# ScalarE's order in the slots that hold a z step: decays, then every z, then back

## The chip, the core and the metric

The kernel runs on one core of a Trainium2 chip. The metric is the device time of one execution in microseconds (us). Five engines work side by side, each through its own list of instructions in order: TensorE (PE, matrix products), VectorE (DVE), ScalarE (ACT), GpSimd (POOL) and SyncE (SP), whose list here is the issue of the DMA transfers. They meet only at semaphores: an instruction that waits holds back everything behind it on its engine.

## The reference, cut to what matters

The input is 64 series of 750 numbers. Each is cut into 10 patches of 128 (hop 64), so there are 640 tokens. All of this is computed, in this order:

```
h  = patches @ W.T + b
hn = rmsnorm(layernorm(h))
z, x, B, C, dt = split(hn @ in_proj.T)
dt = softplus(dt @ dt_proj.T + bias);  dA = exp(dt * A);  dBx = dt * x * B
state = dA * state + dBx               # along the 10 tokens of a series, 16 states per channel
y  = (sum over states of C * state) + D_skip * x
y  = y * silu(z);  m = res + y @ out_proj.T
h  = h + m + (silu(gate) * up) @ down  # on rmsnorm(m)
h  = h + second MLP on layernorm(h)
```

## The kernel before, in words

The tokens are cut into two chunks of 290 (chunk 0) and 350 (chunk 1); channels lie on the 128 partitions in 8 tiles. Everything is fp32. The recurrence is cut into 64 units: units 0 to 31 are chunk 0, units 32 to 63 chunk 1; four units make one tile of channels, and a unit holds four states. Units are the slots of the program: `schedule()` puts other steps beside each unit, and each engine walks the slots on its own.

What one unit costs each engine:

- ScalarE computes four decays `exp(dt*A)` (`decay`, L551) into the four PSUM buffers `da`. The buffers form a ring: decays 0 and 1 of a unit may be written once VectorE has finished the first product (L792) of the unit before, decays 2 and 3 once it has finished the second.
- GpSimd multiplies `dtx` and `bb` (L453) into `hs`; VectorE scans (L781) twice, multiplies by `cb` (L792), scans twice, multiplies. For chunk 0 TensorE then sums the states with an identity matrix (L1000, `state_sum`); for chunk 1 GpSimd adds them.
- After four units VectorE's `gate_y` (L807 and L813 in chunk 0, L810 and L813 in chunk 1) multiplies y by z. It waits for the state sum and for z.

Beside the units of chunk 0 run the projections of its own tiles and then those of chunk 1; beside the units of chunk 1 runs the first half of the work behind the recurrence for chunk 0 (output projection, two MLPs). Products go to a ring of three work banks of PSUM, later four: a product can start once the bank three products back has been read. ScalarE does the steps `dtp` (softplus), `xs`, `in_c` and `in_z` one slot late (`late(slots, 1)`). `in_z` is `silu`, from another table set than `exp`; `preload_act_table_set` loads a set (L528), and where a function of another set follows without one, a load appears at that function's own line (L551, L668).

ScalarE's loop over the slots (around L720) does, for each unit: decays 2 and 3 of this unit, the steps in `first`, decays 0 and 1 of the next unit, the steps in `second`, and a reload of the exp/log set if silu's is in. Where the slot holds `dtp`, `xs` or `in_c`, these are split between the two lists. Where it holds none, `second` is cut in half. That rule meets slots with z alone (4, 8, 12, 24, 28, 32: three z in the first, two in the others) and slots with z beside steps of another kind (37: `rms2` of chunk 0, `ysum` and the z of tile 6; 50: `ln2_mean`, on which ScalarE does nothing, and the z of tile 7). TensorE does slot 37's `rms2` product first in its slot, then that z's product, and then the first MLP; VectorE does `rms2`'s scaling (L864) between its scans.

SyncE issues the loads of `bb` and `cb` two and three units ahead, each when its buffer is free; those of the streamed weights `wraw` begin in slot 30 of its list.

Of the kernel before, what the change touches and what calls it, by code (L numbers as in the profile page):

```python
# [147 lines left out]
def late(slots, lag, kinds=LATE):  # L148
    def lag_of(i, s):
        if i == 1:  # L150
            return min(lag, 2)
        return lag if s[0] in kinds and slots[i][0] is not None and not (s in SEAM and lag == 1) else 0
    return [(unit, [s for j in range(max(0, i - lag), i + 1) for s in slots[j][1] if lag_of(j, s) == i - j])
            for i, (unit, _) in enumerate(slots)]
# [30 lines left out]
def build(nc, patches, tok_w, small, w_in, w_dt, w_stream, out):  # L185
    slots = schedule()
    uses = work_bank_uses()

    readers = [s for _, steps in slots for s in steps if s[0] in ("out", "gu", "down")]
    load_of = {s: i for i, s in enumerate(readers)}  # L190
    split_loads = [i for i, s in enumerate(readers) if s[0] != "out" and s[1] == NCH - 1]
# [4 lines left out]
    with ExitStack() as ctx:  # L196
# [137 lines left out]
        def splits_at(s):  # L334
            if s == ("out", NCH - 1, KD - 2):
                return range(NW - 1)
            if is_split(s) and split_of[s] + NW - 1 < SPLITS:
                return [split_of[s] + NW - 1]
            return []
# [177 lines left out]
        def _(act):  # L517
# [13 lines left out]
            def log_tables():  # L531
                use_tables("natural_log_exp_and_others")
# [5 lines left out]
            def decay(u, p):  # L538
                c, m, q = unit_of(u)
                k, n = piece(u, p), TS[c]  # L540
                if k == 0:
                    act.wait_ge(da_zeroed, 1)
                    act.wait_ge(a_neg_done, 1)
                act.wait_ge(dt_ready, c * KI + m + 1)
                if k >= ND:
                    act.wait_ge(c_times, (k - ND) // 2 + 1)
                src = dt[:, m, 0:n].rearrange("p (b t) -> p b t", t=STEPS)[:, :, 1:]
                for i in range(GS[c]):
                    dst = da[:, k % ND, i * n:(i + 1) * n].rearrange("p (b t) -> p b t", t=STEPS)[:, :, 1:]
                    j = m * NS + q * NQ + p * GS[c] + i  # L550
                    last = nc.scalar.activation(dst, src, ACT.Exp, scale=a_neg[:, j:j + 1])  # L551
                last.then_inc(da_done, 1)

            def split_high(k):
                i = split_loads[k]
                act.wait_ge(w_loaded[i % NRAW], 16 * (i // NRAW + 1))
                if k >= NW:
                    full(act, readers[split_loads[k - NW]])
                nc.scalar.copy(ws[:, k % NW, 0, :], wraw[:, i % NRAW, :]).then_inc(w_hi_done, 1)  # L559
# [151 lines left out]
            for unit, steps in late(slots, 1):  # L711
                if unit == 0:
                    decay(0, 0)
                    decay(0, 1)

                if unit is not None and NP[unit // UNITS] == 4:
                    decay(unit, 2)
                    decay(unit, 3)
                if unit is None:
                    first, second = steps, []  # L720
                else:

                    parts = []
                    for s in steps:
                        if s[0] == "dtp" and s not in SEAM:
                            parts += [("softplus1",) + s[1:], ("softplus2",) + s[1:]]
                        elif s[0] in LATE and s[0] != "in_z" and s not in SEAM:
                            parts.append(s)
                    n = len(parts) // 2
                    first = parts[:n]  # L730
                    second = parts[n:] + [s for s in steps if s[0] == "in_z" and s not in SEAM]
                    second += [s for s in steps if s[0] not in LATE or s in SEAM]
                    if not parts:
                        n = len(second) // 2
                        first, second = second[:n], second[n:]
                for s in first:
                    for k in splits_at(s):
                        split_high(k)
                    step(s)
                if unit is not None and unit + 1 < NCH * UNITS:  # L740
                    decay(unit + 1, 0)
                    decay(unit + 1, 1)
                for s in second:
                    for k in splits_at(s):
                        split_high(k)
                    step(s)
                if tables[0] == "silu_and_others" and unit is not None:
                    log_tables()
# [424 lines left out]
```

## Time and profile before

| | |
|---|---|
| runs | 679.99 us median of 3 (679.35 to 681.1) |
| profiled execution | 679.04 us, of which span 677.1 |
| mean granted TensorE clock | 0.977 of full |
| busy: PE, DVE, ACT, POOL | 632.5, 425.6, 345.3, 429.3 us |
| DMA | 163.51 MB, 241 GB/s over the span |

Times in rows are microseconds from the start of the span. TensorE is busy 93% of the span, the others about half to two thirds; but such shares are means over stages. Up to about 131 us TensorE often waits for others, from 131 to 219 it hardly does, and it pauses at a few places after that. In the rows of the timeline, a number in brackets is the time for which the engine was idle before, with what ended it. In those of the lines view a group of instructions has its count, its busy time, the mean of one in ns, and the idle time before it.

### The profile page before, as it was taken

The numbers are of one execution on the slowest core, as the hardware profiler recorded it, in microseconds if no ns is written. First come the engines' busy times: TensorE is split into PE (matmuls) and PEld (weight loads), VectorE is DVE, ScalarE is ACT, GpSimd is POOL, SyncE is SP. The second block draws the span as 40 slices with busy tenths as digits, with TensorE's granted clock in tenths as the row PEclk, the third lists the DMA queues.
The fourth block names the chain that finished last, engine by engine and source line by source line (L and its number), as shares of the span: only waits on it lengthen the run. The fifth ranks groups of instructions, "written<-read, shape, count | busy, mean of one in ns | idle before, by whom it ended". The sixth has DMA issues, their size and how long they took to land.

```text
span 677.1 us, 8630 instructions
## 1 busy us (share of the span) xinstructions
PE 632.5 (93%) x2846; PEld 506.2 (75%) x2846; DVE 425.6 (63%) x660; ACT 345.3 (51%) x658; POOL 429.3 (63%) x244
## 2 busy tenths in 40 slices
PE   4969997799999889999979999999999999999998
PEld 3637674466665667777757777766999998999998
DVE  4088895899887889889897988861332232332132
ACT  4359989248999364333246333321543443543441
POOL 0276773537777899997877978744455464455561
PEclk9979997899999899999989999999999999999999
DMA  8799997379999969998876989643444344233421
GB/s 337 263 358 345 317 301 259 133 230 369 318 355 348 391 259 340 413 366 317 324 258 218 340 323 314 223 124 99 151 139 142 124 155 126 63 125 131 149 67 44
DMA packets 49165, 163.51 MB, mean 241 GB/s; under 512 B 4320, under 2 KB 18528, under 8 KB 48480
## 3 DMA queue, kind: packets, MB, share of 16 engines
q1 hardware_dynamic: 49120, 162.95, 69.2%
q8 instruction: 23, 0.38, 0.2%
q14 instruction: 22, 0.18, 0.1%
HBM read 145.24 MB, written 17.69 MB: 241 GB/s over the span
## 4 chain that ended last, share of the span: by engine, by line
PE 79%; DVE 9%; ACT 6%; issue 3%; DMA 2%; POOL 1%; SPq 0%; DVEq 0%; ACTq 0%
PE work L990 57%; PE da L990 15%; PE work L1000 6%; DVE da L781 4%; DVE hs L792 2%; ACT da L551 1%; ACT L528 1%; DMA bb<-b_rows 1%; DMA c_rows<-c_rows 1%; DMA sm<-small 1%; DVE a L847 0%; ACT L668 0%; ACT L551 0%; POOL hs L453 0%; DVE sq L864 0%
## 5 line engine op out<-in xcount | busy, mean ns | idle before, releaser
L781 DVE TENSOR_TENSOR_SCAN da<-da,hs 128x290 f32<-128x290 f32 (+1 forms) x256 | 198.2, 817 | 41.6 <-POOL hs L453 20.9
L453 POOL TENSOR_TENSOR hs<-dtx,bb 128x1160 f32<-128x1160 f32 (+1 forms) x64 | 171.2, 2677 | 62.5 <-PE work L1000 50.4
L551 ACT ACTIVATE da<-dt,a_neg 128x261 f32<-128x261 f32 (+1 forms) x256 | 118.4, 495 | 131.0 <-DVE hs L792 130.5
L432 POOL TENSOR_TENSOR ws<-wraw,ws 128x1024 fp32r<-128x1024 f32 x40 | 101.5, 2538 | 92.7 <-ACT ws L559 92.7
L990 PE MATMUL work<-sq,wraw 128*128 128x290 f32 x512 | 126.0, 407 | 1.3 <-DVE sq L880 0.8
L990 PEld LDWEIGHTS work<-sq,wraw 128*128 128x128 f32 x512 | 96.4, 189 | 30.8 <-issue 1.7
L990 PE MATMUL work<-hn,win 128*128 128x290 f32 (+1 forms) x336 | 102.6, 453 | 17.5 <-DVE hn L855 8.0
L792 DVE TENSOR_TENSOR hs<-da,cb 128x580 f32<-128x580 f32 (+1 forms) x128 | 105.2, 822 | 11.2 <-DMA cb<-c_rows 4.5
L990 PEld LDWEIGHTS work<-hn,win 128*128 128x128 f32 x336 | 65.2, 198 | 50.1 <-issue 25.3
L559 ACT CAST ws<-wraw 128x1024 fp32r<-128x1024 f32 x48 | 50.3, 1048 | 70.7 <-PE da L990 34.3
L990 PE MATMUL work<-hn,ws 128*128 128x350 f32 x480 | 79.2, 323 | 1.6 <-DVE hn L951 1.6
L990 PEld LDWEIGHTS work<-hn,ws 128*128 128x128 f32 x480 | 77.3, 189 | 1.9 <-issue 1.9
L1000 PE MATMUL work<-hs,sm 128*128 128x290 f32 x256 | 69.3, 414 | 0.0
L990 PE MATMUL work<-gated_n,wraw 128*128 128x290 f32 x256 | 63.3, 407 | 0.0
L1000 PEld LDWEIGHTS work<-hs,sm 128*128 128x128 f32 x256 | 49.5, 194 | 17.1 <-issue 1.0
L990 PEld LDWEIGHTS work<-gated_n,wraw 128*128 128x128 f32 x256 | 48.4, 189 | 14.2
L990 PE MATMUL da<-hn,ws 128*128 128x350 f32 x288 | 47.5, 323 | 0.0
L990 PE MATMUL da<-gated,ws 128*128 128x350 f32 x288 | 47.0, 323 | 0.0
L990 PEld LDWEIGHTS da<-gated,ws 128*128 128x128 f32 x288 | 46.5, 188 | 0.0
L990 PEld LDWEIGHTS da<-hn,ws 128*128 128x128 f32 x288 | 46.4, 189 | 0.0
L899 DVE TENSOR_TENSOR pair<-th,work 128x350 f32<-128x350 f32 x20 | 10.4, 520 | 56.6 <-PE work L990 50.6
L477 POOL TENSOR_TENSOR acc<-acc,hs 128x700 f32<-128x700 f32 x16 | 26.7, 1667 | 17.3 <-DVE hs L792 17.3
(99 smaller groups left out, 649.0 us busy)
## 6 DMA issues: line engine op xcount, KB each, us to landing
wraw<-w_stream SPq DMA_DIRECT2D x104, 512.0 KB, 3.6
bb<-b_rows SPq DMA_DIRECT2D x32, 700.0 KB, 6.7
cb<-c_rows SPq DMA_DIRECT2D x32, 700.0 KB, 4.7
bb<-b_rows SPq DMA_DIRECT2D x32, 580.0 KB, 8.5
cb<-c_rows SPq DMA_DIRECT2D x32, 580.0 KB, 6.6
c_rows<-c_rows SPq DMA_DIRECT2D x8, 875.0 KB, 11.6
c_rows<-c_rows SPq DMA_DIRECT2D x8, 725.0 KB, 6.9
win<-w_in SPq DMA_DIRECT2D x4, 1024.0 KB, 14.0
```

What stands on the lines that cost most here:

```text
L432: nc.gpsimd.tensor_tensor(ws[:, k % NW, 1, :], wraw[:, split_loads[k] % NRAW, :], ws[:, k % NW, 0, :].bitcast(F32), ALU.subtract).then_inc ...
L453: nc.gpsimd.tensor_tensor(hs[:, u % NH, 0:NQ * n].rearrange("p (n t) -> p n t", t=n), dtx[:, t % 2, 0:n].unsqueeze(1).to_broadcast([P, NQ, ...
L477: nc.gpsimd.tensor_tensor(total, total, lo, ALU.add).then_inc(added, 1)
L528: nc.scalar.preload_act_table_set(name)
L551: last = nc.scalar.activation(dst, src, ACT.Exp, scale=a_neg[:, j:j + 1])
L559: nc.scalar.copy(ws[:, k % NW, 0, :], wraw[:, i % NRAW, :]).then_inc(w_hi_done, 1)
L781: nc.vector.tensor_tensor_scan(da[:, k % ND, 0:w], da[:, k % ND, 0:w], hs[:, u % NH, p * w:(p + 1) * w], 0.0, ALU.mult, ALU.add).then_inc( ...
L792: nc.vector.tensor_tensor(hs[:, u % NH, here].rearrange("p (i w) -> p i w", w=w), da[:, k % ND:k % ND + 2, 0:w], cb[:, u % NC, here].rearr ...
L899: nc.vector.tensor_tensor(gated_f[:, i % 2, 0:n], th[:, i % 2, 0:n], bank((s, "up")), ALU.mult).then_inc(gated_raw, 1)
L990: last = nc.tensor.matmul(dst, w, x, start=(k == 0), stop=(k == len(pairs) - 1))
L1000: last = nc.tensor.matmul(work[SUM][:, 0:n], sm[:, S_IDENT:S_IDENT + P], hs[:, u % NH, i * n:(i + 1) * n], start=(q == 0 and i == 0), stop ...
```

## The change

The halving of `second` is left out where it contains an `in_z` step.

```
@@ -730,7 +730,7 @@
                     first = parts[:n]
                     second = parts[n:] + [s for s in steps if s[0] == "in_z" and s not in SEAM]
                     second += [s for s in steps if s[0] not in LATE or s in SEAM]
-                    if not parts:
+                    if not parts and not any(s[0] == "in_z" for s in second):
                         n = len(second) // 2
                         first, second = second[:n], second[n:]
```

Only ScalarE's list is altered; those of the other four engines are the same, word for word. On ScalarE, slot 8 and the decays around it stand in the program before as follows (`da` are decays, `z` the silu of a z tile, each ACT_TABLE_LOAD a change of table set).

```order
L652 COPY xf<-work 128x290
L551 ACTIVATE da<-dt,a_neg 128x29x9 x2
L528 ACT_TABLE_LOAD
L668 ACTIVATE z<-work 128x290
L551 ACT_TABLE_LOAD
L551 ACTIVATE da<-dt,a_neg 128x29x9 x2
L668 ACT_TABLE_LOAD
L668 ACTIVATE z<-work 128x290
L528 ACT_TABLE_LOAD
L551 ACTIVATE da<-dt,a_neg 128x29x9 x2
```

And this is the same slot of ScalarE in the changed program.

```order
L652 COPY xf<-work 128x290
L551 ACTIVATE da<-dt,a_neg 128x29x9 x4
L528 ACT_TABLE_LOAD
L668 ACTIVATE z<-work 128x290 x2
L528 ACT_TABLE_LOAD
L551 ACTIVATE da<-dt,a_neg 128x29x9 x2
```

Decays 0 and 1 of unit 9 have moved ahead of the first z, and two of the four table loads are gone. The six slots with z alone change in this way, and 12 of the program's 37 table loads go. Slot 37 changes too, without a load more or less: here is ScalarE's list there as a difference (`sq` are the squares of `rms2`, L592 and L593 its inverse root, L661 `ysum`; the rows of L551 are the decays of units 37 and 38).

```order
 L642 COPY c_rows<-work 128x350
-L551 ACTIVATE da<-dt,a_neg 128x35x9 x2
+L551 ACTIVATE da<-dt,a_neg 128x35x9 x4
 L586 ACTIVATE sq<-a 128x290 x4
 L592 ACTIVATE rstd_ln<-work,cols 128x290
 L593 ACTIVATE work<-rstd_ln 128x290
-L551 ACTIVATE da<-dt,a_neg 128x35x9 x2
 L661 ACTIVATE work<-xf,sm 128x350
```

Decays 0 and 1 of unit 38 now stand ahead of the squares, on which TensorE's next product depends. In slot 50 nothing moves, since its other step has no ScalarE instruction.

## Rows read from the trace of the kernel before

**Rows 1.** The page: the chain that ended last, shares of the span by engine.

```profile
PE 79%; DVE 9%; ACT 6%; issue 3%; DMA 2%; POOL 1%; SPq 0%; DVEq 0%; ACTq 0%
```

**Rows 2.** The chain in order of time: start, length, what.

```profile
101.63 1.28 ACT L528
...
131.29 8.88 PE work L990 x24
...
244.20 98.39 PE work L990 x400
```

**Rows 3.** Lines of ScalarE: count, busy us, mean ns, idle before.

```profile
L528 ACT ACT_TABLE_LOAD x25 | 32.1, 1283 | 4.2 <-PE work L990 3.1 <-PEq L1167 0.7
```

**Rows 4.** Timeline, slot 8 and what follows it, four engines.

```profile
75.75 0.76 DVE L792 TENSOR_TENSOR hs<-da,cb 128x580 f32<-128x580 f32 x1
...
76.83 0.41 ACT L668 ACTIVATE z<-work 128x290 f32<-128x290 f32 x1
...
78.55 0.88 ACT L551 ACTIVATE da<-dt,a_neg 128x261 f32<-128x261 f32 x2
...
78.85 2.12 PE L990 MATMUL work<-hn,win 128*128 128x290 f32 x8
...
79.13 1.42 DVE L781 TENSOR_TENSOR_SCAN da<-da,hs 128x290 f32<-128x290 f32 x2 [0.50 <-ACT da L551]
...
80.81 2.12 PE L1000 MATMUL work<-hs,sm 128*128 128x290 f32 x8
...
82.99 1.42 DVE L781 TENSOR_TENSOR_SCAN da<-da,hs 128x290 f32<-128x290 f32 x2 [1.57 <-ACT da L551]
...
85.12 0.51 DVE L807 SCALAR_TENSOR_TENSOR work<-xf,sm,work 128x290 f32<-128x290 f32 x1
```

**Rows 5.** Timeline, VectorE in slot 12 (unit 13).

```profile
103.44 1.42 DVE L781 TENSOR_TENSOR_SCAN da<-da,hs 128x290 f32<-128x290 f32 x2 [1.57 <-ACT da L551]
```

**Rows 6.** Timeline, slot 4 (unit 5) up to its gate.

```profile
62.43 2.12 PE L1000 MATMUL work<-hs,sm 128*128 128x290 f32 x8
...
64.66 0.53 DVE L807 SCALAR_TENSOR_TENSOR work<-xf,sm,work 128x290 f32<-128x290 f32 x1 [0.32 <-PE work L1000]
```

**Rows 7.** Timeline, slot 28 (unit 29) up to its gate.

```profile
194.31 2.12 PE L1000 MATMUL work<-hs,sm 128*128 128x290 f32 x8
...
195.52 1.42 DVE L781 TENSOR_TENSOR_SCAN da<-da,hs 128x290 f32<-128x290 f32 x2 [1.61 <-ACT da L551]
...
197.66 0.52 DVE L807 SCALAR_TENSOR_TENSOR work<-xf,sm,work 128x290 f32<-128x290 f32 x1
```

**Rows 8.** Timeline, the end of chunk 0's recurrence and the output projection.

```profile
217.93 0.89 DVE L792 TENSOR_TENSOR hs<-da,cb 128x700 f32<-128x700 f32 x1 [3.65 <-DMA cb<-c_rows]
...
222.34 17.58 PE L990 MATMUL work<-yg,wraw 128*128 128x290 f32 x64 [3.33 <-issue]
```

**Rows 9.** Timeline, slot 37.

```profile
242.71 0.98 ACT L551 ACTIVATE da<-dt,a_neg 128x315 f32<-128x315 f32 x2
...
243.62 1.43 ACT L586 ACTIVATE sq<-a 128x290 f32<-128x290 f32 x4
...
244.06 0.89 DVE L792 TENSOR_TENSOR hs<-da,cb 128x700 f32<-128x700 f32 x1
...
244.20 2.19 PE L990 MATMUL work<-sq,mean_w 128*128 128x290 f32 x8 [1.92 <-ACT sq L586]
```

**Rows 10.** Timeline, TensorE behind three other pauses.

```profile
48.45 5.83 PE L990 MATMUL work<-hn,win 128*128 128x290 f32 x16 [1.65 <-ACT xf L652]
...
114.36 3.63 PE L1000 MATMUL work<-hs,sm 128*128 128x290 f32 x8
...
351.73 4.20 PE L990 MATMUL work<-sq,mean_w 128*128 128x290 f32 x8 [4.85 <-ACT sq L586]
```

**Rows 11.** Windows: us, busy us of PE, PEld, DVE, ACT, POOL, granted clock, DMA share, GB/s.

```profile
86.00:96.00 10.00, 9.53 (x39) 6.61 (x38) 9.72 (x15) 8.41 (x23) 6.93 (x6) 1.00 0.94 288
...
112.00:120.00 8.00, 8.00 (x21) 5.44 (x22) 2.38 (x5) 6.44 (x13) 1.84 (x1) 0.66 0.53 199
```

More of the change, by code:

```diff
@@ L732, in _ @@
                     second += [s for s in steps if s[0] not in LATE or s in SEAM]
-                    if not parts:
+                    if not parts and not any(s[0] == "in_z" for s in second):
                         n = len(second) // 2
```

## The prediction, made before the changed kernel had run

> **What bounds the kernel now.** I read the chain that ended last first. It is TensorE for 79% of the span and ScalarE for only 6% [rows 1], so a load saved on ScalarE counts only where ScalarE is on the chain. In order of time the chain shows where that is: table loads lie on it in slots 8 and 12 (the one of slot 12 is in [rows 2]), and from 131.29 to 219 us it is TensorE's products alone. Then the lines of ScalarE: a table load takes 1283 ns [rows 3]; 25 stand at L528 and six each at L551 and L668, with the same mean. Last the timeline of each slot whose order changes, with two questions: who waits for ScalarE, and what would be late next.
>
> **Slots 8 and 12: the gain.** In slot 8 VectorE waits twice for decays of unit 9, 0.50 us and 1.57 us [rows 4]. The two groups of decays stand behind one load, a z, a load, and behind a load, a z, a load. In the new order decays 0 and 1 of unit 9 wait only for the product of 75.75, which ends at 75.75 + 0.76 = 76.51. They take 0.88, to 77.4. A load (1.28), two z of 0.41 and a load follow: 78.7, 79.5, 80.8. The first of decays 2 and 3 is written 0.44 later and a scan can start at about 81.35. VectorE's side: the first scans of unit 9 start unhindered at 78.6 and last 1.42, the product 0.76, so the third scan is wanted at 80.8 and waits 0.5 for its decay. It starts at 81.35 instead of 82.99: 1.6 us earlier, and so do the product behind it and the gate of 85.12, now ready at 83.5.
>
> What would be late next is TensorE. The first z is now read at 79.2 instead of 77.24 (76.83 + 0.41), and the product at 78.85 needs its bank: it starts some 0.4 late. The state sum of 80.81, for which the gate waits, then ends at 80.81 + 2.12 + 0.4 = 83.35. That is just ahead of 83.5, so the gate keeps its 1.6, with nothing to spare. Slot 12 has the same wait of 1.57 at 103.44 [rows 5] and the same pattern: again 1.6. Two slots: 3.2 us. From there to 131.29 the chain runs through VectorE, ScalarE and low-clock TensorE in sequence, so this shift reaches the end of it whole.
>
> **Slot 4: nothing, or a little back.** Here VectorE's next gate starts at 64.66 when the state sum ends at 62.43 + 2.12 = 64.55 [rows 6]. TensorE sets that time, so earlier decays give nothing. The first z frees its bank about 2 us later here too, which is just when TensorE's next product wants it: 0 to 0.3 lost, I take 0.1. Early part in sum: 3.2 - 0.1 = 3.1 us gained.
>
> **Slots 24, 28 and 32: covered by TensorE.** In slot 28 VectorE waits 1.61 at 195.52, and the gate starts at 197.66 [rows 7]. The state sum that it needs ends at 194.31 + 2.12 = 196.43, so the gate can move up by at most 1.1, and TensorE, which has no pause in this stretch, gains nothing. The first z is read some 1.8 later, still before TensorE wants its bank, so it loses nothing in 24 and 28; in slot 32 I expect a stall of 0 to 0.9, just ahead of a pause that swallows it.
>
> **The pause at 219.** Before the output projection TensorE is idle 3.33 us until chunk 0's last gate, which stands behind a product that waits 3.65 for a `cb` transfer until 217.93 [rows 8]. That load is issued when VectorE has finished a product, 1.1 earlier in the new order; but the engines of DMA are nearly full (0.94 of their time in a stretch of the early part [rows 11], and no less here), so it lands earlier by less than it is issued earlier. Between 0 and 1.1: I take 0.6. The clock behind this pause: 64 products took 17.58, where at full clock eight take 2.12 with their tail. A shorter pause may keep the clock, but VectorE and GpSimd, not TensorE, then set slot 37, so I count nothing.
>
> **Slot 37: what is given back.** This is not a slot of z alone, and no load goes there. TensorE waits from 242.28 (244.20 - 1.92) for the squares of `rms2`, which ScalarE starts at 243.62 behind the decays of 242.71 [rows 9]. In the new order two more decays stand ahead of them, and these wait for VectorE's product of 244.06, which ends at 244.95; 0.97 for the decays, and the squares start at 246.0 instead of 243.62. That is 2.3 us on the path of TensorE, whose whole first MLP waits behind that product. After it TensorE is on the chain without a break to 342.6 [rows 2], so no pause makes this up.
>
> The pause grows from 1.92 to 4.2 us, and then there is TensorE's clock. The restart of 244.20 ran at 2.4 GHz (eight products in 2.19), while that behind 4.85 of idle ran at 1.2 GHz (eight in 4.20) and so did one behind 1.65 (sixteen in 5.83) [rows 9, 10]. So a pause of 4.2 will bring the low clock: the difference of the eight products alone is 4.20 - 2.19 = 2.0. But since 1.65 of idle was once enough, I take it that some executions of the kernel before also pay this at 244.20, and the profiled one did not; it is 0.95 quicker than the median of the runs (679.04 against 679.99). Against the profiled execution slot 37 costs 2.3 + 2.0 = 4.3, against the median about 2.3 + 1.0 = 3.3.
>
> The Trainium skill, page "TensorE: Matmul & The Clock Gate", section "Part 1: The HAM clock gate", says that activity releases a throttle and that where its windows fall differs from run to run. The rows agree in that 1.92 kept the clock and 1.65 lost it. By that rule the clock's part is not a fixed price but a draw in every execution, of both kernels.
>
> **The restart near 112.** The clock also falls before 112 (0.66 over 112 to 120 [rows 11]), and the eight products of a state sum took 3.63 there [rows 10] instead of 2.12. The pauses ahead of it shrink a little in the new order. If it held in every run, the state sum would save 1.5 and the products beside it about 0.8: 2.3 us. I give that 0.3 in the mean.
>
> **The sum.** Against the profiled execution: -3.1 - 0.6 + 4.3 = +0.6, so 679.6. Against the median: -3.1 - 0.6 + 3.3 = -0.4, less 0.6 for the restarts that sometimes keep the clock: -1.0, so 679.0. I take the second, since the result will be a median.
>
> The Trainium skill, page "ScalarE: Activation LUTs", section "What ACT_TABLE_LOAD costs", prices a change of set at 1283 ns for the load and about 1380 ns for a drain. The trace agrees on the load and shows no drain: the z of 76.83 ends at 77.24 and the decays, with a load between, start at 78.55 [rows 4], 1.31 later. By the page's 2.66 us each saved pair would be worth 2.8 us more to ScalarE, and slots 8 and 12 would give more than the whole wait that VectorE has there; I go by the rows.
>
> **The rivals.**
>
> - *Slot 37 does not take it back.* If VectorE's product there (244.06) comes earlier relative to TensorE, or the clock holds behind the pause, or the restart at 112 keeps the clock in most runs, the early gain shows. For: the gain rests on plain waits. Against: the pause of 4.2 is longer than any that kept the clock. Time: 679.99 - 3.7 + 2.3 - 2.3 = 676.3 with both clocks kept, 677.9 with less.
> - *Slower: slot 37's pause decides, the early gain is lost.* The place is the bank ring: if TensorE's product of 78.85 starts more than 0.5 late, the state sum and not VectorE sets the gate at 85.12, and each further tenth comes off the gain in slots 8 and 12; at 1.6 late they give nothing. DMA, at 0.94, could do the same when the units come quicker: from a share of 1.0 on the gain is capped at 6% of a stretch of 20 us, 1.2. With the early gain at 1 and slot 37 at its full 4.3: +3.3, so 683.3. For: both margins are tenths of a us. Against: the worked start is 0.4 late, and loads are issued two units ahead.
> - *The change does nothing on the path.* ScalarE's 12 loads (15.4 us) go, but where it waits for VectorE anyway. Against: two waits of 1.57 on the chain. Time 680.0, inside the forecast.
>
> **How the numbers follow.** What a measurement of this kernel can tell from no change is 0.3%, 2.0 us: below 677.95 is faster, above 682.0 slower. The forecast, early gain and slot 37 nearly cancelling (677.95 to 682), has 0.47 with the third rival in it. The first rival has 0.38, the second 0.15. The range 675.8 to 682.4 leaves out about 0.1 on either side.
>
> **What would show it.** Right: 12 loads fewer at 1283 ns, none at L551 or L668; VectorE's waits in units 9 and 13 about 0.5 each; everything at 131 us about 3.1 earlier; VectorE's gate in unit 29 just behind the state sum; the squares of slot 37 behind four decays, TensorE idle about 4.2 ahead of them and restarting at a granted clock of 0.5. Wrong: TensorE idle behind z banks in units 8 and 12 for over 0.5; a pause in slot 37 of 2 us or less; a new wait for `cb` or `bb` before 131; TensorE pausing between 131 and 210.

## The result, and the profile after

The kernel after takes 677.36 us, the median of 13 runs (675.95 to 680.32); the kernel before, on the same chip, takes 680.0 (677.67 to 682.2). The ratio is 0.9962, with a 95% interval of 0.9946 to 0.9978: 2.6 us less, where 1.0 less was forecast. The profiled execution took 676.66 us, its span is 674.7 and its mean granted clock 0.979. Below, every gain in us that is taken from a ratio is what the ratio lacks to 1, times 680.

| | before | after |
|---|---|---|
| profiled execution, span | 679.04, 677.1 | 676.66, 674.7 |
| busy: PE, DVE, ACT, POOL | 632.5, 425.6, 345.3, 429.3 | 630.5, 425.5, 329.3, 428.9 |
| mean granted clock | 0.977 | 0.979 |

ScalarE's busy time falls by 16.0 us, the 12 loads saved (12 x 1.283 = 15.4) and little else. From the lines view of the kernel after (count, busy us, mean ns, idle before), L528 and L551, with no load left elsewhere; then L551 from the page of the kernel before:

```profile
L528 ACT ACT_TABLE_LOAD x25 | 32.1, 1283 | 5.1 <-PE work L990 4.0 <-PEq L1167 0.7
...
L551 ACT ACTIVATE da<-dt,a_neg 128x261 f32<-128x261 f32 (+1 forms) x256 | 118.4, 495 | 144.7 <-DVE hs L792 144.5
```

```profile
L551 ACT ACTIVATE da<-dt,a_neg 128x261 f32<-128x261 f32 (+1 forms) x256 | 118.4, 495 | 131.0 <-DVE hs L792 130.5
```

The decays wait 13.7 us longer for VectorE: most of the 16.0 has become waiting. So the count of loads says nothing of the time; the places where another engine waits for ScalarE do. First slot 8, the timeline of the kernel after (start, length, what, idle before), as in [rows 4]:

```profile
77.02 0.88 ACT L551 ACTIVATE da<-dt,a_neg 128x261 f32<-128x261 f32 x2 [1.09 <-DVE hs L792]
...
77.92 1.28 ACT L528 ACT_TABLE_LOAD   x1
...
78.96 1.41 DVE L781 TENSOR_TENSOR_SCAN da<-da,hs 128x290 f32<-128x290 f32 x2
...
79.21 0.72 ACT L668 ACTIVATE z<-work 128x290 f32<-128x290 f32 x2
...
79.77 2.19 PE L990 MATMUL work<-hn,win 128*128 128x290 f32 x8 [0.33 <-ACT z L668]
...
79.94 1.28 ACT L528 ACT_TABLE_LOAD   x1
...
81.24 0.88 ACT L551 ACTIVATE da<-dt,a_neg 128x261 f32<-128x261 f32 x2
...
81.75 1.42 DVE L781 TENSOR_TENSOR_SCAN da<-da,hs 128x290 f32<-128x290 f32 x2 [0.52 <-ACT da L551]
81.80 2.12 PE L1000 MATMUL work<-hs,sm 128*128 128x290 f32 x8
...
84.02 0.53 DVE L807 SCALAR_TENSOR_TENSOR work<-xf,sm,work 128x290 f32<-128x290 f32 x1
```

Decays, load, both z, load, decays: VectorE's first scans of unit 9 no longer wait and the third waits 0.52 instead of 1.57 [rows 4]. TensorE stands 0.33 for the z bank, and its state sum ends at 83.92, just ahead of the gate. The same in slot 12, where before had 103.44 and 1.57 [rows 5], and then the restart of TensorE that the chain shows at 131.29 before [rows 2]:

```profile
100.70 1.42 DVE L781 TENSOR_TENSOR_SCAN da<-da,hs 128x290 f32<-128x290 f32 x2 [0.52 <-ACT da L551]
...
110.85 2.12 PE L1000 MATMUL work<-hs,sm 128*128 128x290 f32 x8
...
126.27 5.99 PE L990 MATMUL work<-hn,win 128*128 128x350 f32 x11 [4.48 <-DVE hn L855]
```

The scan of slot 12 is 2.7 us earlier, the restart 5.0. What lies between is the clock: the state sum takes 2.12, where before one took 3.63 [rows 10], and over 112 to 120 us the granted clock is that of 2.4 GHz, 1.00, instead of 0.66 [rows 11]. Windows view of the kernel after (busy time of each engine, then the granted clock, DMA share and GB/s):

```profile
112.00:120.00 8.00, 8.00 (x32) 5.80 (x32) 5.06 (x10) 5.73 (x12) 4.91 (x3) 1.00 0.38 139
```

From 190 us on, the timeline of the kernel after:

```profile
191.46 3.16 SPq L395 DMA_DIRECT2D wraw<-w_stream  x6
...
192.46 0.52 DVE L807 SCALAR_TENSOR_TENSOR work<-xf,sm,work 128x290 f32<-128x290 f32 x1 [1.39 <-PE work L1000]
...
207.58 2.63 PE L990 MATMUL work<-hn,win 128*128 128x350 f32 x8 [1.11 <-ACT z L668]
...
211.87 0.89 DVE L792 TENSOR_TENSOR hs<-da,cb 128x700 f32<-128x700 f32 x1 [3.11 <-DMA cb<-c_rows]
...
216.32 15.89 PE L990 MATMUL work<-yg,wraw 128*128 128x290 f32 x64 [0.45 <-issue]
```

The gate of unit 29 now waits 1.39 for the state sum, TensorE stands 1.11 for a z bank, VectorE still waits 3.11 for `cb`; yet TensorE's pause before the output projection has shrunk from 3.33 to 0.45, and its 64 products take 15.89 instead of 17.58 [rows 8]. The projection starts 6.0 us earlier than before and ends 7.7 earlier (232.21 against 222.34 + 17.58 = 239.92). Then slot 37 takes most of that back, as against [rows 9]:

```profile
235.96 0.97 ACT L551 ACTIVATE da<-dt,a_neg 128x315 f32<-128x315 f32 x2 [0.84 <-DVE hs L792]
...
237.63 0.89 DVE L792 TENSOR_TENSOR hs<-da,cb 128x700 f32<-128x700 f32 x1
...
238.61 0.97 ACT L551 ACTIVATE da<-dt,a_neg 128x315 f32<-128x315 f32 x2 [1.68 <-DVE hs L792]
...
239.52 1.43 ACT L586 ACTIVATE sq<-a 128x290 f32<-128x290 f32 x4
...
240.10 4.12 PE L990 MATMUL work<-sq,mean_w 128*128 128x290 f32 x8 [5.52 <-ACT sq L586]
```

ScalarE waits for VectorE's product of 237.63 with the second pair of decays, and the squares stand behind it. TensorE is idle 5.52 us and restarts at 1.2 GHz (a granted clock of 0.50 over 240 to 244 us; 4.12 for the eight products against 2.19). The squares' products end 2.2 us earlier than before (244.22 against 246.39), and the span is 2.4 shorter: from slot 37 on, nothing more is won or lost.

### The profile page after: what moved, and what is told of

It reads as the page before. It is cut to its first block, busy times and chain, and to the rows that moved or that the text cites. A ratio compares the mean times of both kernels' runs of the same rounds, so it can differ in the third digit from the quotient of the medians.

```text
span 674.7 us, 8618 instructions
## 1 busy us (share of the span) xinstructions
PE 630.5 (93%) x2846; PEld 505.2 (75%) x2846; DVE 425.5 (63%) x660; ACT 329.3 (49%) x646; POOL 428.9 (64%) x244
## 4 chain that ended last, share of the span: by engine, by line
PE 73%; DVE 12%; ACT 4%; POOL 4%; issue 3%; DMA 2%; SPq 0%; DVEq 0%; ACTq 0%; POOLq 0%
PE work L990 53%; PE da L990 15%; DVE da L781 7%; PE work L1000 5%; DVE hs L792 3%; POOL hs L453 2%; ACT L528 1%; DMA bb<-b_rows 1%; ACT da L551 1%; DMA c_rows<-c_rows 1%; DMA sm<-small 1%; POOL acc L479 0%; POOL acc L477 0%; POOL hs L466 0%; DVE a L847 0%
## 5 line engine op out<-in xcount | busy, mean ns | idle before, releaser
L781 DVE TENSOR_TENSOR_SCAN da<-da,hs 128x290 f32<-128x290 f32 (+1 forms) x256 | 198.1, 817 | 35.1 <-POOL hs L453 21.2
L551 ACT ACTIVATE da<-dt,a_neg 128x261 f32<-128x261 f32 (+1 forms) x256 | 118.4, 495 | 144.7 <-DVE hs L792 144.5
L1000 PE MATMUL work<-hs,sm 128*128 128x290 f32 x256 | 67.8, 408 | 0.0
L899 DVE TENSOR_TENSOR pair<-th,work 128x350 f32<-128x350 f32 x20 | 10.4, 520 | 56.7 <-PE work L990 50.6
```

The source lines that it names most:

```text
L781: nc.vector.tensor_tensor_scan(da[:, k % ND, 0:w], da[:, k % ND, 0:w], hs[:, u % NH, p * w:(p + 1) * w], 0.0, ALU.mult, ALU.add).then_inc( ...
L899: nc.vector.tensor_tensor(gated_f[:, i % 2, 0:n], th[:, i % 2, 0:n], bank((s, "up")), ALU.mult).then_inc(gated_raw, 1)
L1000: last = nc.tensor.matmul(work[SUM][:, 0:n], sm[:, S_IDENT:S_IDENT + P], hs[:, u % NH, i * n:(i + 1) * n], start=(q == 0 and i == 0), stop ...
```

## The experiments

All were timed beside the kernel before. "z slots" are the six slots with z alone. The first edit is shown against the kernel after, the next three against the kernel before.

**The six z slots alone** (slot 37 in the old order):

```
-                    if not parts and not any(s[0] == "in_z" for s in second):
+                    if not parts and not all(s[0] == "in_z" for s in second):
```

> The six slots that hold z alone are changed, slot 37 is as in the kernel before. Theory (slot 37 takes back part of an early gain): 2.3 to 4.3 us below the changed kernel, so about 673 to 675, with the squares of rms2 behind two decays and TensorE idle 2 to 3.2 us ahead of them. Rival (slot 37's move costs nothing, the net of the change is just what slots 8 and 12 give): the same 677.4 as the changed kernel.

Measured: 675.24 us, ratio 0.9922 (0.9897 to 0.9947), 5.3 us less. Timeline of this kernel:

```profile
212.79 0.89 DVE L792 TENSOR_TENSOR hs<-da,cb 128x700 f32<-128x700 f32 x1 [3.23 <-DMA cb<-c_rows]
...
238.25 3.67 PE L990 MATMUL work<-sq,mean_w 128*128 128x290 f32 x8 [2.81 <-ACT sq L586]
```

The z slots give 5.3, and the change gives up 2.7 of it in slot 37 (the intervals of this kernel and of the kernel after just touch; the next run shows the cost of slot 37 clear of noise). Even here the pause in slot 37 is longer than before (2.81) and the clock falls, so some of the gain is lost there in any case.

**Slot 37 alone** (the z slots in the old order):

```
-                    if not parts:
+                    if not parts and unit != 37:
```

> Only slot 37 is changed: decays 0 and 1 of unit 38 stand ahead of the squares, all z slots as in the kernel before. Theory: 2.3 us for the squares and up to 2.0 for the clock behind a pause of 4.2 us, so 682.3 to 684.3. Rival: 680, no difference.

Measured: 684.27 us, ratio 1.0055 (1.0033 to 1.0078), 3.7 us more, near the 3.3 of the prediction. Its timeline:

```profile
220.23 0.89 DVE L792 TENSOR_TENSOR hs<-da,cb 128x700 f32<-128x700 f32 x1 [4.86 <-DMA cb<-c_rows]
...
247.74 0.97 ACT L551 ACTIVATE da<-dt,a_neg 128x315 f32<-128x315 f32 x2 [1.35 <-DVE hs L792]
...
248.65 1.43 ACT L586 ACTIVATE sq<-a 128x290 f32<-128x290 f32 x4
...
249.23 3.88 PE L990 MATMUL work<-sq,mean_w 128*128 128x290 f32 x8 [4.25 <-ACT sq L586]
```

A pause of 4.25 where 4.2 was worked out, and 3.88 where 4.20 was taken for the restart. One line that moves no load into the slot costs half a per cent.

**The early slots alone and the late slots alone.** `if not parts and unit not in (4, 8, 12):` and `if not parts and unit not in (24, 28, 32):`; the units named take the new order, all others, slot 37 among them, keep the old.

> Only slots 4, 8 and 12 are changed. Theory: the chain of VectorE is 3.1 us shorter up to 106 us, more where the clock then holds at the restart near 112: 674.5 to 677. Rival (the gain is made in slots 24 to 32, at the transfer before the output projection): near 680.

> Only slots 24, 28 and 32 are changed. Theory: TensorE covers them; VectorE's product before chunk 0's last gate comes 0.6 to 1.1 earlier, so 679 to 679.5, within what can be told from no change. Rival: 2 us or more, below 678.

Measured: early 677.41, ratio 0.9957 (0.9939 to 0.9974), 2.9 less; late 678.5, ratio 0.9963 (0.9943 to 0.9983), 2.5 less. Together 5.4, which is the 5.3 of the z slots: the two parts add. The early part came out just above the expected range (677.41 against 677). The late part was expected at 0.5 to 1 us; its interval leaves 1.2 to 3.9, so by the ratio it is the rival of this run (2 us or more) that came true, though the median of 678.5 is not below its 678. Early alone:

```profile
214.69 0.89 DVE L792 TENSOR_TENSOR hs<-da,cb 128x700 f32<-128x700 f32 x1 [4.82 <-DMA cb<-c_rows]
...
241.23 2.19 PE L990 MATMUL work<-sq,mean_w 128*128 128x290 f32 x8 [1.92 <-ACT sq L586]
```

Late alone (its profiled execution, 680.85 us, is the second slowest of its 12 runs, so only its waits are read, not its moments):

```profile
219.46 0.89 DVE L792 TENSOR_TENSOR hs<-da,cb 128x700 f32<-128x700 f32 x1 [3.64 <-DMA cb<-c_rows]
...
244.53 3.88 PE L990 MATMUL work<-sq,mean_w 128*128 128x290 f32 x8 [2.40 <-ACT sq L586]
```

With the late slots in the old order the wait for `cb` in unit 33 is 4.82 and 4.86, and 3.65 in the profiled execution of the kernel before. In the new order it is 3.64, 3.23 and 3.11 here, and 2.78 to 3.94 over all seven profiles that have the six weight loads where they were. So the two groups overlap, and what can be said is that the same order gave 3.65 once and 4.86 once. TensorE's pause before the output projection does separate them: 3.33, 4.49 and 4.53 in the old order, 0.45 to 1.24 in the new. Part of that is no gain: in slot 32 TensorE now stands 1.11 for a z bank, and so reaches the pause later.

**What the wait for `cb` hangs on.** The kernel before, with two of the six first weight loads where they were and four issued behind the `cb` load of unit 35:

```
+                if unit == UNITS + 1:
+                    for i in range(2, NRAW):
+                        load_w(i)
...
                     if s == ("in_z", 1, 2):
-                        for i in range(NRAW):
+                        for i in range(2):
                             load_w(i)
```

> The kernel before, except that of the six weight loads which SyncE issues in slot 30 only two stay there, and four follow the cb load of unit 35. Question: why slots 24, 28 and 32 gave 2.5 us and not 0.6. Theory (the cb load of unit 33 stands in the DMA rings behind 3 MB of weights, and the earlier product of unit 29 sends these off earlier): VectorE's wait for cb in unit 33 goes from 3.7 to 4.9 to below 1, TensorE's pause before the output projection shrinks by about 3 and the clock holds: 676.5 to 678. Rival (the bytes of all loads together set it): the wait stays, 680.4.

Measured: 677.09 us, ratio 0.995 (0.9934 to 0.9967), 3.4 us less, with ScalarE's order untouched. Timeline:

```profile
199.01 0.91 SPq L395 DMA_DIRECT2D wraw<-w_stream  x2
...
213.63 1.88 SPq L395 DMA_DIRECT2D wraw<-w_stream  x4
...
215.25 0.89 DVE L795 TENSOR_TENSOR hs<-da,cb 128x700 f32<-128x700 f32 x1
...
241.47 2.19 PE L993 MATMUL work<-sq,mean_w 128*128 128x290 f32 x8 [2.14 <-ACT sq L589]
```

The product that waited (L795 here) waits no more. So the transfer was late because six weight loads of 512 KB stood ahead of it, in a stretch where DMA is full (a share of 1.03 over 204 to 212 us of the kernel before). This bears on why the late slots pay. They let VectorE run ahead inside unit 29 while the gate is held by the state sum. The weight loads stand in SyncE's list behind a load of `cb` that waits for VectorE's product, not for the gate; so in the kernel after they leave 1.0 us before the gate (191.46 against 192.46), in the kernel before 0.5 behind its start of 197.66 [rows 7]:

```profile
198.13 3.10 SPq L395 DMA_DIRECT2D wraw<-w_stream  x6
```

The rest follows them: from the first of the six loads to the product that waits for `cb` it is 19.8 to 21.2 us in all ten profiles that have the six together, whatever the order of the slots.

**Slot 37 with TensorE kept busy.** The kernel after, with 16 products of `mean_w` with itself, 128 columns wide, written into the bank that the squares' product then overwrites; no result depends on them:

```
+                    if s == ("rms2", 0):
...
+                        for _ in range(16):
+                            nc.tensor.matmul(bank(s)[:, 0:P], mean_w[:, :], mean_w[:, :], start=True, stop=True)
```

> The changed kernel with 16 products of 128 columns on TensorE in slot 37's pause, ahead of the rms2 product and into its bank, which that product then overwrites: some 3.5 us of work in a pause of 4.2 to 5.5. Nothing waits for them. Theory (the pause costs also by the clock behind it): 1.5 to 2.0 us below the changed kernel's 677.4, so 675.4 to 675.9, and the rms2 product's eight matmuls in about 2.2 instead of 4.1. Rival (only the wait counts, slot 37 costs 2.7 by that alone): 677.4.

Measured: 677.04 us, ratio 0.9944 (0.9923 to 0.9965), against 0.9962 for the kernel after. Timeline (L1058 is the filling; the trace has 32 records for its 16 products):

```profile
237.78 3.73 PE L1058 MATMUL work<-mean_w 128*128 128x128 f32 x32
...
242.11 1.43 ACT L586 ACTIVATE sq<-a 128x290 f32<-128x290 f32 x4
...
242.68 2.19 PE L990 MATMUL work<-sq,mean_w 128*128 128x290 f32 x8 [1.17 <-ACT sq L586]
```

The profile shows the effect: the pause before the squares' product is 1.17 and the eight products take 2.19 instead of 4.12. That is 1.9 for the eight products; over all runs the gain is 1.2 with overlapping intervals, less than the 1.5 to 2.0 that was expected, and this execution with the clock held was the slowest of its seven (677.65). So the filling keeps the clock, but that the low clock is a part of slot 37's price in the median is not shown.

**The squares first.** The z slots alone, and in slot 37 the squares ahead of decays 2 and 3:

```
+                if ("rms2", 0) in steps:
+                    squares("rms2", 0, res_done)
                 if unit is not None and NP[unit // UNITS] == 4:
                     decay(unit, 2)
```

> As the kernel with only the z slots changed (675.2), and slot 37's squares also stand ahead of decays 2 and 3 of unit 37. Theory (each pair of decays ahead of the squares costs TensorE its wait and its length): the squares start 1.0 to 2.4 us sooner, the pause falls below 2 us: 672.5 to 674.2. Rival (VectorE or GpSimd sets that place, TensorE's start does not matter): 675.2.

Measured: 673.63 us, ratio 0.9901 (0.9876 to 0.9926), which is 1.4 below the z slots alone, inside what was expected, with overlapping intervals. Timeline:

```profile
238.97 1.45 ACT L586 ACTIVATE sq<-a 128x290 f32<-128x290 f32 x4
...
239.56 2.19 PE L993 MATMUL work<-sq,mean_w 128*128 128x290 f32 x8 [1.03 <-ACT sq L586]
```

The pause is 1.03, less than in the kernel before, and the clock holds.

**The same idea in slot 50.** The z slots alone, with `ln2`'s squares in the place of tile 7's z and that z one slot later: in slot 50 `squares("ln2", 0, centered2)` where `step(("in_z", 1, 7))` stood, and this behind `inverse_root`.

> As the kernel with only the z slots changed (675.2); in slot 50 the squares of ln2 (which stood in slot 51 behind two table loads, the z of tile 7 and two decays) take the place of that z, and the z follows the inverse root in slot 51. Theory (the same fault as in slot 37: TensorE idles 4.85 us ahead of the squares): squares 4 us earlier, the pause about 1, the clock held: 4 to 6 us below, 669.5 to 671.5. Rival (VectorE's scans of unit 51 or the bank that the late z holds become the bound): 673 to 675.

Measured: 675.78 us, ratio 0.9926 (0.9903 to 0.995): no gain over the z slots alone, where 4 to 6 us were expected; the rival's 673 to 675 is near. The 12 runs spread from 671.96 to 680.29, and the profiled one is the slowest, so only its waits are read. Timeline:

```profile
349.66 2.19 PE L996 MATMUL work<-sq,mean_w 128*128 128x290 f32 x8 [2.04 <-ACT sq L586]
...
352.49 0.42 ACT L593 ACTIVATE work<-rstd_ln 128x290 f32<-128x290 f32 x1
...
355.88 1.54 DVE L886 TENSOR_TENSOR sq<-a,work 128x290 f32<-128x290 f32 x4
...
356.47 9.88 PE L996 MATMUL work<-sq,wraw 128*128 128x290 f32 x27 [4.03 <-DVE sq L886]
```

The first pause did shrink (2.04, clock held, against 4.85 and the low clock in [rows 10]). But VectorE's scaling, ready to start at 352.91, stands in its list behind the whole of unit 51 and starts at 355.88. The pause behind it is 4.03, where the z slots alone have 1.10; the two pauses together are 6.07 here and 5.95 there, so nothing is won. Half of the edit was missing, on another engine.

**All that helps, without and with slot 50.** The first has the z slots, the squares first and the weights later. The second adds the slot 50 edit with its other half: VectorE's scaling fourth in unit 51's list, and the exp set loaded right behind the z.

> Only the z slots changed, slot 37's squares first, and four of the six weight loads later. Theory (the z slots' late part and the weights shorten the same pause before the output projection, so their gains overlap): 0.5 to 1.5 below 673.7, so 672.2 to 673.2. Rival (separate causes, gains add): 3.4 below, 670.3.

> As the one with both, and slots 50 and 51: the squares of ln2 ahead of the z of tile 7, that z behind the inverse root with no load more than before, and on VectorE the scaling of ln2 behind the first product of unit 51 instead of behind the whole unit. Theory (in the first try at slot 50 VectorE's order took back what ScalarE's gave): TensorE's pause there falls from 4.9 us to about 2, then a stall of 1 to 3 us for the first tanh: 1.5 to 4 below the one with both, 668.5 to 671.5. Rival (the tanh behind tile 7's softplus takes all of it): 672.5.

Measured: 671.75 us, ratio 0.9868 (0.9848 to 0.9887); and 670.06, ratio 0.9847 (0.9827 to 0.9866). First the last gate of chunk 0 in the first kernel, then the timeline of the second:

```profile
214.83 0.52 DVE L813 SCALAR_TENSOR_TENSOR work<-xf,sm,work 128x290 f32<-128x290 f32 x1 [2.86 <-PE work L1006]
```

```profile
340.80 2.19 PE L1006 MATMUL work<-sq,mean_w 128*128 128x290 f32 x8 [2.04 <-ACT sq L589]
...
345.11 8.05 PE L1006 MATMUL work<-sq,wraw 128*128 128x290 f32 x32 [1.53 <-DVE sq L893]
...
354.15 4.14 PE L1006 MATMUL work<-sq,wraw 128*128 128x290 f32 x16 [0.99 <-DVE gate L946]
```

The first gains 9.0 where its parts, each alone, gain 6.7 and 3.4. The median is just below the expected range, and the interval (7.7 to 10.3) holds their sum of 10.1 as well, so the time does not tell overlap from addition. The profile does: the wait for `cb` is gone, but now the gate waits 2.86 for the state sum, and the projection starts at 215.95, only 0.4 earlier than in the kernel after, as does the restart near 126. Up to there the weights add nothing that can be seen to the z slots: both remove the same wait.

The second is 1.4 lower again, with intervals that overlap. Both pauses in slots 50 and 51 are short now, but TensorE then stands 0.99 for the first gate of the MLP. At 0.9847 it is the fastest of all, 10.4 us below the kernel before.

**The kernel after again** (unchanged).

> The changed kernel once more beside the runs of this call: 677.4, within 0.3% either way; theories do not differ.

Measured: 677.71 us, ratio 0.9956 (0.994 to 0.9972). The first result stands.

## Why the forecast came out 1.6 us too high

Term by term, in us gained over the median of the kernel before (the experiments each have an interval of 1 us or more to either side):

| term | prediction | runs |
|---|---|---|
| early slots, with the restart near 112 | 3.1 + 0.6 | 2.9 |
| late slots | 0.6 | 2.5 |
| slot 37 | -3.3 | -2.7 (taken from the z slots alone) |

The 1.6 are the errors of three terms that partly cancel, so that the forecast came this near is in part luck. The measured 677.36 lies inside the range but below the 677.95 down to which the prediction counted its forecast, on the ground of its first rival (0.38). That rival has the result right and the reasons mostly not: VectorE's product in slot 37 comes later relative to TensorE (3.1 us behind the start of its pause, 1.8 before) and the clock falls behind that pause; only the restart near 112 went as it says, and the early slots gave no more for it.

*Early slots: right.* Worked out was 1.6 in each of slots 8 and 12, and TensorE some 0.4 late, with the state sum just ahead of the gate. The scans went from 1.57 to 0.52, TensorE was 0.33 late, the state sum ended 0.10 ahead of the gate, and slot 12's scan came 2.7 us earlier in an execution that was already some 0.2 behind at 48 us: 2.9 of the 3.2. Slot 4 gave nothing, as said: its gate starts at 65.08 instead of 64.66, of which 0.2 is that execution's lag.

*The restart near 112: mis-sized.* It got a chance of 0.3. Over 112 to 120 us the granted clock was:

| early slots | granted clock over 112 to 120 us, one figure for each profile |
|---|---|
| old order | 0.66 (before), 0.79 (slot 37 alone), 0.60 (late alone), 0.62 (weights later) |
| new order | 1.00 in seven, 0.80 (squares first), 0.79 (slot 50) |

Seven of nine against none of four. Of the pauses ahead of it two are gone (1.33 before 104.76 and 0.47 before 107.43 in the kernel before), the third is 1.26 instead of 1.88, and only the last is longer (0.87 against 0.59): they do not only "shrink a little". In the kernel after this is the difference between 2.7 us at slot 12 and 5.0 at the restart.

What becomes of the 5 us is seen in the profile of the early slots alone. Its restart is 5.2 earlier than before (126.07 against 131.29), TensorE reaches the pause before the projection 4.4 earlier (219.10 - 4.49 = 214.61 against 219.01), but VectorE then waits 4.82 for `cb` instead of 3.65, and the projection starts only 3.2 earlier. In these two profiles that wait takes up what the clock gave, and 2.9 are left over all runs. In the kernel after TensorE reaches the pause at 216.32 - 0.45 = 215.87, 3.1 earlier than before, since it has also stood 1.11 in slot 32.

*The pause at 219: the term that was furthest off.* The prediction took 0.6 for it and nothing for the clock behind it. The late slots, which it priced at that, gave 2.5. Two things were wrong. The first is when the loads are issued: the prediction had them 1.1 earlier, as far as the gate can move, but what they wait for is the product ahead of the gate, and that ends 1.39 before the gate starts (191.07 against 192.46), where it ended just behind the gate's start before. The second is the clock: with a pause of 0.45 to 1.24 instead of 3.33 to 4.53, TensorE keeps 2.4 GHz over the projection. Window 216 to 232 of the kernel after, then of the one with the early slots alone:

```profile
216.00:232.00 16.00, 15.68 (x64) 12.24 (x65) 13.06 (x19) 4.59 (x10) 15.61 (x11) 1.00 1.03 399
```

```profile
216.00:232.00 16.00, 12.90 (x45) 9.78 (x46) 13.75 (x20) 6.61 (x15) 13.89 (x10) 0.79 1.03 392
```

The reason given for counting nothing was that VectorE and GpSimd set slot 37. They do: the projection ends 7.7 earlier in the kernel after, the squares come only 4.1 earlier, and TensorE waits longer for them (5.52, where 4.2 was worked out). The profile of the z slots alone against that of the early slots alone shows what the late slots bring by themselves. The restart near 126, ahead of the late slots, comes 1.1 later in the first:

```profile
127.17 9.12 PE L990 MATMUL work<-hn,win 128*128 128x350 f32 x22 [4.49 <-DVE hn L855]
```

```profile
126.07 9.70 PE L990 MATMUL work<-hn,win 128*128 128x350 f32 x24 [4.49 <-DVE hn L855]
```

So all moments are taken from there. The weight loads go 2.6 earlier (192.25 against 193.73), the product that waits for `cb` is 3.0 earlier (212.79 against 214.69), the squares' product starts 4.1 earlier (238.25 against 241.23), and since its clock falls, it ends 2.6 earlier (241.92 against 243.42), which is the 2.5 of the runs. By these rows the earlier transfer is the larger part, and a part comes back as low clock in slot 37. No run here holds the one fixed and changes the other, so the division stays open.

*Slots 24, 28 and 32: right in kind.* The gate of unit 29 waits for the state sum as worked out, and slot 32 stalls by 1.11, a little over the 0.9 that was given as the end. (By the prediction's last paragraph a pause of TensorE between 131 and 210 was a sign of being wrong; this one had been worked out, and the pause behind it did swallow it.) That loads are issued earlier was foreseen too; what was missed is that this matters by what stands ahead of them in SyncE's queue.

*Slot 37: right.* 3.3 expected against the median, 3.7 measured when made alone, 2.7 when taken from the z slots alone. Four decays ahead of the squares, a pause of 4.25, a restart at the low clock: each step is in the rows. What no run shows is the reason for taking 1.0 and not 2.0 for the clock, that some executions of the kernel before already pay it at 244.20.

*The clock as a draw.* The Trainium skill, page "TensorE: Matmul & The Clock Gate", section "Part 1: The HAM clock gate", says that where the throttle's windows fall differs from run to run, and the prediction made a draw of every restart from it. The profiles agree in part. Near 112 it was a draw: in all nine profiles with the early slots in the new order TensorE has the same pauses there (0.34, 1.26 and 0.87, within 0.01), and the clock held in seven and fell in two. At slot 37 it was none: in all 13 profiles the outcome followed the length of the pause, as the last section lists.

## What to carry to other kernels

When an edit regroups work on an in-order engine, look for the instruction that another engine's pause hangs on and count everything that is now ahead of it: a table switch saved in six slots was half paid back in a seventh that had no switch to save. Read a wait for a transfer by the queue ahead of it as well as by its issue: six large loads left over 20 us before their data was used, and moving four of them gained 3.4 us, no less than the change studied here. And do not size a term from one wait in one execution; two kernels with the same order in that stretch showed 4.8 where the profile in hand showed 3.65.

## What the runs showed of the hardware

TensorE's clock behind a pause was steadier at one place than the prediction allowed. In slot 37 the eight products behind the pause took 2.19 us after pauses of 1.03 (three profiles), 1.17, 1.92 (two, that of before among them) and 2.14, and 3.67 to 4.20 after pauses of 2.40, 2.81, 2.90, 4.25, 5.52 and 5.53. In slot 50 a pause of 2.04 kept the clock in both profiles that had it, and one of 4.85 lost it in the eleven others. But this does not carry to other places. Near 48 us a pause of 1.65 lost it [rows 10], where TensorE had stood idle for 5.79 some 10 us before and restarted at the low clock (eight products in 3.85), while ahead of slot 37's pause it had worked some 20 us without a pause. No run tells whether that is the reason. And near 112 pauses that are alike to 0.01 us (1.26 and 0.87) were followed by a granted clock of 1.00 over 112 to 120 in seven profiles and of 0.80 and 0.79 in two.

The small transfer behind a burst of large ones came at a fixed distance: 19.8 to 21.2 us from the first of six loads of 512 KB to the product that waited for the `cb` load behind them, in ten profiles; with four of the six moved behind it, no wait was left.
